# An attention and mixture-of-experts layer: a constant moved between two exponentials, waits of the expert stage put elsewhere, output transfers issued after the next quarter's loads

## The reference

```python
xn = _layernorm(x, axis=-1)
x = x + attn(xn, Wq, Wk, Wv, Wo, bo) + ffn(xn, gate_weight, ...)
...
# attn: 16 heads of 64, 8 key/value heads
energy = einsum('nqhd,nkhd->nhqk', q, k) - slopes * |i - j|
attn = softmax(energy / sqrt(64));  out = attn @ v;  return out @ Wo.T + bo
...
# ffn: 32 routed experts, top 6 of 4 of 8 groups, plus two shared halves
scores = sigmoid(xf @ gate_weight.T)
combine = (top-6 scores, normalised) * 2.5, zero elsewhere
for every expert:  acc += combine[:, e] * ((silu(xf @ gu[:I].T) * (xf @ gu[I:].T)) @ dn.T)
shared = (silu(xf @ sg.T) * (xf @ su.T)) @ sd.T
```

## Time and profile before

| What | Value |
|---|---|
| Median of 2 runs | 10741.5 us (10741.21 to 10741.8) |
| The profiled execution, its own time | 10752.67 us |
| Its span, first to last instruction, slowest core (5) | 10751.1 us |
| Spans of the eight cores | 10727.1 to 10751.1 us |
| Mean granted TensorE clock of the cores | 0.940 to 0.942 |
| TensorE busy | 8851.2 us (82%) |
| ScalarE busy | 3562.6 us (33%) |
| VectorE busy | 4556.2 us (42%) |

### The profile page before, as it was taken

How to read it: one execution, slowest core, us unless ns; L and a number is a source line. 1 busy time by engine, 2 the same in 40 slices (tenths; PEclk the granted TensorE clock), 3 DMA queues, 4 the chain that set the end, 5 groups by cost and what they waited for, 6 DMA issues and landing times.

```text
span 10751.1 us, 126162 instructions; the slowest of 8 cores (10727.1 to 10751.1 us)
## 1 busy us (share of the span) xinstructions
PE 8851.2 (82%) x39713; PEld 3361.2 (31%) x39713; DVE 4556.2 (42%) x7526; ACT 3562.6 (33%) x4327; POOL 350.2 (3%) x504
## 2 busy tenths in 40 slices
PE   2178778778778769999978999997999997999998
PEld 1022222222222223333333333333333333333333
DVE  6425445445445434444433444442444442444443
ACT  3148878778778751111101111111111111111110
POOL 1000000000000000000000000000000000000000
PEclk9988888888888889999999999998999998999999
DMA  3020010110110024444443433443443443443342
GB/s 95 4 52 12 26 34 8 31 34 5 33 34 4 27 53 69 71 66 65 71 87 67 71 67 64 70 71 83 71 68 66 67 71 84 70 71 66 64 71 65
DMA packets 324944, 593.57 MB, mean 55 GB/s; under 512 B 12992, under 2 KB 96960, under 8 KB 324288
## 3 DMA queue, kind: packets, MB, share of 16 engines
q0 software_dynamic: 226096, 450.99, 25.0%
q1 hardware_dynamic: 98224, 134.51, 4.0%
HBM read 986.08 MB, written 33.55 MB: 95 GB/s over the span
## 4 chain that ended last, share of the span: by engine, by line
PE 67%; ACT 13%; DVE 8%; issue 7%; DMA 4%; DVEq 1%; ACTq 0%; SPq 0%; POOL 0%; POOLq 0%
PE dn_ps L835 19%; PE g_ps L813 18%; PE u_ps L813 17%; ACT e_sb L629 9%; DVE p_sb L658 4%; PE o_ps L583 3%; PE st_ps L559 2%; PE o_ps L586 2%; DMA xq_sb<-xn_scr 1%; DMA x_t<-x 1%; PE qp_ps L529 1%; PE wo_ps L784 1%; ACT Bp L618 1%; DMA ot_sb<-o_scr 1%; DVE h_sb L905 1%
## 5 line engine op out<-in xcount | busy, mean ns | idle before, releaser
L835 PE MATMUL dn_ps<-h_sb,dn_sb 128*128 128x512 bf16 x8704 | 2067.7, 378 | 383.9 <-DVE h_sb L913 190.2
L629 ACT ACTIVATE e_sb<-st_ps,negE_sb 128x1024 bf16<-128x1024 f32 x2048 | 2223.1, 1114 | 180.4 <-PE st_ps L564 136.3
L658 DVE TENSOR_TENSOR p_sb<-e_sb,Bp 128x1024 bf16<-128x1024 bf16 x2048 | 1417.2, 692 | 1378.8 <-ACT e_sb L629 1301.1
L905 DVE SCALAR_TENSOR_TENSOR h_sb<-u_ps,silu_sb 128x512 bf16<-128x512 f32 x1088 | 752.5, 692 | 2943.8 <-PE u_ps L813 2943.3
L813 PE MATMUL g_ps<-xnh,gu_sb 128*128 128x512 bf16 x8704 | 1968.7, 379 | 4.7 <-PE dn_ps L835 4.7
L813 PE MATMUL u_ps<-xnh,gu_sb 128*128 128x512 bf16 x8704 | 1967.4, 379 | 0.0
L922 DVE TENSOR_TENSOR acc<-dn_ps,acc 128x512 f32<-128x512 f32 x2176 | 1503.8, 692 | 879.4 <-PE dn_ps L835 879.3
L883 ACT ACTIVATE silu_sb<-g_ps 128x512 bf16<-128x512 f32 x1088 | 649.9, 597 | 2801.1 <-PE g_ps L813 2801.1
L835 PEld LDWEIGHTS dn_ps<-h_sb,dn_sb 128*128 128x128 bf16 x8704 | 712.8, 96 | 1738.7 <-issue 1179.0
L813 PEld LDWEIGHTS u_ps<-xnh,gu_sb 128*128 128x128 bf16 x8704 | 851.6, 98 | 1027.0
L813 PEld LDWEIGHTS g_ps<-xnh,gu_sb 128*128 128x128 bf16 x8704 | 840.5, 98 | 1045.5 <-issue 50.5
(11 more groups left out here) (111 smaller groups left out, 2633.1 us busy)
## 6 DMA issues: line engine op xcount, KB each, us to landing
gu_sb<-guT POOLq DMA_DIRECT2D x136, 2048.0 KB, 15.3
dn_sb<-dnT POOLq DMA_DIRECT2D x136, 1024.0 KB, 9.0
xq_sb<-xn_scr SPq DMA_DIRECT2D x64, 1024.0 KB, 6.1
xt<-x SPq DMA_DIRECT2D x32, 512.0 KB, 3.9
x_t<-x SPq DMA_DIRECT2D x32, 512.0 KB, 4.4
out<-out_sb SPq DMA_DIRECT2D x32, 512.0 KB, 2.9
xn_scr<-XnT POOLq DMA_DIRECT2D x64, 128.0 KB, 3.5
o_scr<-o_nm POOLq DMA_DIRECT2D x128, 64.0 KB, 2.0
```

The source lines that it names most:

```text
L629: s.activation(e_sb[step % 2][:], st_ps[step % 2][:, :], AF.Exp, bias=self.negE_sb[:, :], scale=0.125).then_inc(self.s_ee, 1)
L658: v.tensor_mul(p_sb[step % 2].ap().rearrange("p (b q) -> p b q", b=2), e_sb[step % 2].ap().rearrange("p (b q) -> p b q", b=2), Bp.ap()[:, ...
L835: i = t.matmul(dn_ps[nd % 2][:, :], dn_sb[gg % 2].ap()[:, cc, fc * 128:(fc + 1) * 128], h_sb.ap()[:, cc, tt * 512:(tt + 1) * 512], start=( ...
L905: i = v.scalar_tensor_tensor(h_sb.ap()[:, cc, sl], u_ps.ap()[:, sl], 1.0, silu_sb.ap()[:, sl], ALU.mult, ALU.mult)
```

## The change

Four things. In the attention, the constant -4 moves from the exponential of the scores (2048 instructions, which then have no bias tile) to the exponential of the distance penalty (128 instructions, which then read `negE_sb`). In the expert stage `h_sb` has two buffers; the down tiles are emitted by a helper `emit_down`, which waits for `h_sb` and the weights once, in front of the first tile, and for `s_acc` in front of each; TensorE's waits for its own matmuls and both no-operations are gone, and GpSimd waits for the matmuls' semaphores instead. `pend` is set and read nowhere: the down tiles of an expert stand directly behind its own up matmuls, as before. `ot_sb` has two buffers. SyncE's queue loads `xnh` and both halves of `ot_sb` for a quarter as soon as the last up matmul of the quarter before is done, and issues the `x_t` loads and stores of that quarter behind them.

```diff
                                      self.D.ap()[:, seg * 1024:(seg + 1) * 1024],
-                                     AF.Exp, scale=-SLOPES[hh] / 8.0)
+                                     AF.Exp, bias=self.negE_sb[:, :],
+                                     scale=-SLOPES[hh] / 8.0)
...
                         s.activation(e_sb[step % 2][:], st_ps[step % 2][:, :],
-                                     AF.Exp, bias=self.negE_sb[:, :], scale=0.125
+                                     AF.Exp, scale=0.125
                                      ).then_inc(self.s_ee, 1)
...
-        h_sb = self.sb(c2, "h_sb", [128, 4, QT1], BF16)
+        h_sb = [self.sb(c2, f"h_sb{i}", [128, 4, QT1], BF16) for i in range(2)]
...
-        ot_sb = self.sb(c2, "ot_sb", [128, NIC, 512], BF16)
+        ot_sb = [self.sb(c2, f"ot_sb{i}", [128, NIC, 512], BF16) for i in range(2)]
...
                 if gg >= 2:
-                    g.wait_ge(self.s_gue, gg - 1)
+                    g.wait_ge(self.s_gmm, 8 * (gg - 1))
+                    g.wait_ge(self.s_umm, 8 * (gg - 1))
...
                 if gg >= 2:
-                    g.wait_ge(self.s_dme, gg - 1)
+                    g.wait_ge(self.s_dmm, 16 * (gg - 1))
...
+            def emit_output_dmas(q):
+                for tc in range(8):
+                    nt = 8 * q + tc
+                    if nt >= 4:
+                        s.wait_ge(self.s_oadd, 2 * nt - 6)
+                    s.dma_start(out=x_t[nt % 4][:],
...
+                    s.wait_ge(self.s_oadd, 2 * nt + 2)
+                    s.dma_start(out=self.out[q * QT1 + tc * 128:
...
             for qd in range(NQ1):
                 if qd >= 1:
-                    for sq in s_outq:
-                        s.wait_ge(sq, 16 * 2 * qd)
+                    s.wait_ge(self.s_gmm, 8 * NE * qd)
+                    s.wait_ge(self.s_umm, 8 * NE * qd)
...
                 for half in range(2):
-                    if half == 1:
-                        s.wait_ge(self.s_wom, 8 * (2 * qd + 1))
-                    s.dma_start(out=ot_sb[:],
+                    if qd >= 1:
+                        s.wait_ge(self.s_wom, 8 * 2 * qd)
+                    s.dma_start(out=ot_sb[half][:],
...
+                if qd >= 1:
+                    emit_output_dmas(qd - 1)
+            emit_output_dmas(NQ1 - 1)
...
+            def emit_down(P, k):
+                fc, tt = k // 2, k % 2
+                self._nd += 1
+                nd = self._nd
+                if k == 0:
+                    t.wait_ge(self.s_hsc, 8 * (P + 1))
+                    t.wait_ge(s_dn[P % 2], 16 * (P // 2 + 1))
+                if nd > 2:
+                    t.wait_ge(self.s_acc, nd - 2)
...
-                    t.wait_ge(self.s_umm, nh_)
-                    t.nop().then_inc(self.s_gue, 1)
-                    t.wait_ge(s_dn[gg % 2], 16 * (gg // 2 + 1))
...
-                            if nd > 2:
-                                t.wait_ge(self.s_acc, nd - 2)
-                            t.wait_ge(self.s_hsc, nh_)
...
-                    t.wait_ge(self.s_dmm, nd)
-                    t.nop().then_inc(self.s_dme, 1)
-                t.wait_ge(self.s_acc, nd)
+                                k += 1
+                    for kk in range(16):
+                        emit_down(gg, kk)
+                    pend = gg
+                t.wait_ge(self.s_acc, self._nd)
```

More of the change, by code:

```diff
@@ L770, in _ @@
             t.wait_ge(self.s_bo, 16 * 9)
-            nd = 0
+            self._nd = 0
             nh_ = 0
             nsil = 0
+            def emit_down(P, k):
[7 more added lines that the diff above has]
+                    t.wait_ge(self.s_acc, nd - 2)
+                for cc in range(4):
+                    i = t.matmul(dn_ps[nd % 2][:, :],
+                                 dn_sb[P % 2].ap()[:, cc, fc * 128:(fc + 1) * 128],
+                                 h_sb[P % 2].ap()[:, cc, tt * 512:(tt + 1) * 512],
+                                 start=(cc == 0), stop=(cc == 3))
+                i.then_inc(self.s_dmm, 1)
             for qd in range(NQ1):
@@ L785, in _ @@
                                          wo_sb.ap()[:, hc, fc * 128:(fc + 1) * 128],
-                                         ot_sb.ap()[:, hc, :],
+                                         ot_sb[half].ap()[:, hc, :],
                                          start=(hc == 0), stop=(hc == 7))
                         i.then_inc(self.s_wom, 1)
+                pend = None
                 for e in range(NE):
@@ L804, in _ @@
                             i.then_inc(self.s_cmm, 1)
+                    k = 0
                     for cc in range(4):
@@ L823, in _ @@
                                     nh_ += 1
-                    t.wait_ge(self.s_umm, nh_)
-                    t.nop().then_inc(self.s_gue, 1)
-                    t.wait_ge(s_dn[gg % 2], 16 * (gg // 2 + 1))
-                    for fc in range(NIC):
-                        for tt in range(2):
-                            nd += 1
-                            if nd > 2:
-                                t.wait_ge(self.s_acc, nd - 2)
-                            t.wait_ge(self.s_hsc, nh_)
[L834 to L839, removed]
-                    t.wait_ge(self.s_dmm, nd)
-                    t.nop().then_inc(self.s_dme, 1)
-                t.wait_ge(self.s_acc, nd)
+                                k += 1
[3 more added lines that the diff above has]
+                t.wait_ge(self.s_acc, self._nd)
                 for tc in range(8):
@@ L890, in _, with emit_add @@
             vs_outq = [self.s_out, self.s_out2, self.s_out3, self.s_out4]
-            nd = 0
+            self._vnd = 0
             nh_ = 0
+            def emit_add():
+                self._vnd += 1
+                nd = self._vnd
+                fc, tt = ((nd - 1) % 16) // 2, (nd - 1) % 2
+                v.wait_ge(self.s_dmm, nd)
+                sl = slice(tt * 512, (tt + 1) * 512)
+                v.tensor_tensor(acc.ap()[:, fc, sl], dn_ps[nd % 2][:, :],
+                                acc.ap()[:, fc, sl], ALU.add
+                                ).then_inc(self.s_acc, 1)
             for qd in range(NQ1):
@@ L904, in _ @@
                             v.wait_ge(self.s_umm, nh_)
-                            i = v.scalar_tensor_tensor(h_sb.ap()[:, cc, sl],
+                            i = v.scalar_tensor_tensor(h_sb[gg % 2].ap()[:, cc, sl],
                                                        u_ps.ap()[:, sl], 1.0,
@@ L912, in _ @@
                                     v.wait_ge(self.s_ce, 2 * (qd * NRE + e + 1))
-                                i = v.tensor_mul(h_sb.ap()[:, cc, sl],
-                                                 h_sb.ap()[:, cc, sl],
+                                i = v.tensor_mul(h_sb[gg % 2].ap()[:, cc, sl],
+                                                 h_sb[gg % 2].ap()[:, cc, sl],
                                                  ce_bc[gg % 2].ap()[:, sl])
                             i.then_inc(self.s_hsc, 1)
[L917 to L924, removed]
+                    for _ in range(16):
+                        emit_add()
                 for tc in range(8):
```

6 lines of the change are left out of this document (added).

## The result

The changed kernel is 2.7% faster: the ratio to the kernel before is 0.9728, with a 95% interval of 0.9707 to 0.975. Against 10741.5 us that is 10449 us; its profiled execution took 10438.8.

What follows compares the result with a forecast made beforehand. Bounds: a three-step ring in the attention, TensorE with waits in the experts, transfers at quarters' ends. From 10752.7, terms -43, -158, -22 and -43 give 10486.7; less 11.2 to the runs' median, 10476 us, range 10400 to 10555.

Steps and rivals of the forecast that it cites:

- The ring of three: Attention: p_sb, value matmul, scores, exponential close after three steps in 3.26 us; a shorter exponential gives a third per step.
- Rival 1: Attention: ScalarE sets the pace, every exponential gives its 92 ns, -176 us instead of -43, 10343 us; chance 0.04.
- The step that failed: Attention: slow TensorE paces a block's first 9 us, with 7 exponentials; only the other 25 or so steps gain 31 ns.
- The down tiles: Expert stage: only waits change, +0.21, -0.735 and -0.65 us in front of, within and behind the tiles; together -158 us.
- The middle term: Within the down tiles: one satisfied wait of 0.105 us goes at 7 stalls of an expert, -0.735 us; other 8 tiles hide it.
- Rival 2: Behind the down tiles: the drain stays, the -0.65 is given back, +81 us, 10557 us; chance 0.11.
- two buffers for `h_sb` do nothing: Expert stage: they save nothing, since VectorE begins the next expert's h_sb long after the last down matmul.
- The first quarter: First projection: the second half's ot_sb, issued with the first, saves 20 us of waiting and some 2 of slow clock: -22.
- The borders: Three later quarters: second ot_sb wait and slow start go, -8 each; projection starts about 6 us earlier; -14 per quarter.
- Rival 3: Quarters' ends: x_t lands 55 us after the issue or more, leaving 19 us of 43 or less, 10500 to 10520; chance 0.08.
- rival 4: Expert stage: denser work lowers TensorE's clock; 5% slow matmuls cancel the 266 us gain, 10% make 11024 us; chance 0.03.
- one sign that the prediction named: Expert windows: a granted clock below 1.00 would show the prediction wrong.

Runs made afterwards that it cites:

- exponentials alone: The kernel before with only the constant moved between the two exponentials; 10681.5 us, attention 3145.1.
- the wait for `h_sb`: The changed kernel with the wait for h_sb put last in front of the first down tile; experts 6107 to 6109 us, 34 less than 6142.5.
- all three edits: The changed kernel with attention waits reordered, the h_sb wait last and x_t loaded four tiles ahead; 10174.9 and 10177.5 us, 10172.6 when repeated.

## Why the prediction was right or wrong

The direction holds, and so do the size (faster by over 2%) and the mechanism of each stage but one. Of the time, 10476 was forecast; the comparison gives 10449 and the profiled execution 10438.8, 27 to 37 us lower and within 10400 to 10555. The attention alone accounts for 21 of the 40 us by which the stages together beat the forecast.

- **The ring of three** was right where the clock is up. A change of 90 ns in it gave 30.5 ns a step (exponentials alone), a wait of 105 ns put in cost 35, and 190 ns of waits taken out gave 64. Rival 1, ScalarE as the bound, is refuted: 64 us instead of 176. The rule of the Trainium skill on the price of a bias ("ScalarE: Activation LUTs", section "What ACT_TABLE_LOAD costs") stood the test as a duration, with 90 and 93 ns here; booking it on each instruction would have been wrong.
- **The step that failed** is that in a block's first 9 us "TensorE, slow after the pause between blocks, sets the pace there", so that only "the other 25 or so steps" gain. Forecast 43 for the attention, measured 64. The last 23 steps gave 45 us and the first eight 25, of which the forecast had 4 at most; the pauses between the blocks of a pair gave 4 instead of 6, and those between pairs, with `Bp`, cost 8 instead of 12. Two things stand behind the 25 us.

  The exponential is partly in the path there too. Sort the 448 blocks of the eight cores that follow another block of their pair by how many pairs of score matmuls run before the clock is up. Blocks with six such pairs took 11.13 us for their first eight steps before and 10.94 after, blocks with five 10.57 and 10.21. By this sorting some 14 of the 25 us are gained in blocks of the same kind, the first blocks of the pairs included. That is an estimate.

  The other 11 come from blocks in which the clock rises earlier: five pairs in 48 blocks before and in 162 after, six in 363 and 215. The stretch at the lower level, which begins in the pause ahead of the block, is 10.2 us long in 433 of the 448 blocks before and in 365 after; in 15 and 81 it is 6.8. Over a block's first 9 us the mean granted clock rose from 0.52 to 0.56. One block of core 1 as a window, from its first score matmul on as in the earlier trace rows:

```profile
1192.07:1201.07 9.00, 7.46 (x30) 1.88 (x29) 4.75 (x7) 6.82 (x8) 1.06 (x2) 0.62 0.07 15
```

  The kernel with the exponentials alone has the same shift (165 blocks with five pairs), so that edit is its cause; by which path a shorter exponential makes the clock rise earlier was not tried and is open.
- **The down tiles.** Forecast +0.21, -0.735 and -0.65 us an expert; measured +0.211, -0.86 and -0.634 (medians of the 124 routed experts with a routed one behind). The middle term had one price of a wait too few: 0.86 is eight times 0.107. The seven long pauses of the median expert shrank by 0.106 us each, as forecast; what is left lies in the short pauses between the other tiles, which the forecast took as hidden. The sum, -163 against -158, was right, although it has the 4 us of the clock against it that are told at the wait for `h_sb`. Rival 2, the drain that stays, is refuted by the missing idle time, and putting the wait back shows its price of 0.52.
- **That two buffers for `h_sb` do nothing** is shown by the kernel with one: 6142.6 against 6142.5.
- **The first quarter**: forecast -22, measured -23.
- **The borders**: forecast -14 each, measured -18. Each projection starts 9.0 us earlier instead of 6, since `x_t` came 36.5 us after the loads instead of the 40 I took, and takes 8.6 us less, as against 8. Rival 3 did not come about.
- **The clock**: in the executions compared the clock of an expert's window is 1.00 after as before, so rival 4 did not come about in its size. But one sign that the prediction named, a clock below 1.00 in the expert stage, did appear, in 18 stretches of 3.4 us. They follow longer pauses and not, as rival 4 had it, a denser stage. What rival 4 says against itself, that eight cores run dense at 1.00, holds for the executions compared and not for all of them.

## What to carry to other kernels

Follow one result around until it comes back before you price an edit: here the ring closed after three steps, so anything in it was worth a third, and the one wait put outside it nothing. Put the wait that is satisfied last at the end of a list of waits, and the others ahead of it; two reordered lists in the attention and one in the expert stage gave another 1.5% without a byte or an operation changed. When a transfer queue is reordered, look at what now stands behind the large loads, and issue small loads that are needed sooner ahead of them.

## What the runs showed that I had not expected

- The clock comes up earlier in more blocks when the exponential is shorter by 90 ns; that is worth an estimated 11 of the 64 us gained in the attention.
- A longer pause in front of the down tiles costs more than its length: behind pauses of 2.0 to 2.2 us the clock fell for 3.4 us, 18 times on eight cores. The kernel before, with pauses of 1.8 us at most, has none.
- VectorE started 0.35 us late in every 31st step of the attention (63 of 2048 on core 5) in the kernel before, and so in the changed kernel and with the exponentials alone. Once its wait for `e_sb` stood last, it did so in none of the last 23 steps of the blocks. Why is open.
- SyncE's instruction that issues a transfer can itself stand for long. In the changed kernel two issues of `ot_sb` took 17.09 us and the load of `x_t` behind them 10.60; with all three edits they took 16.11 and the store behind them 12.85. Four loads of 1 MB were under way each time. Such a queue delays not only what lands but what is issued.
